# First attention and its projection in one block, with the rotary products in PSUM

## The reference

```python
qkv = x @ Wqkv                                   # q, k, v
q = x_q * cos + rotated(x_q) * sin               # the same for k
att = softmax(where(causal, (q @ k.T) * scale, -inf))
out = (att @ v) @ Wo + bo
x = layernorm(x + out)
```

## Time and profile before

| | us |
|---|---|
| median of three runs | 849.43 (847.52 to 850.48) |
| profiled execution | 850.17 |
| its span, first to last instruction | 848.5 |
| first product on DVE (chunk 0) | 8.97 |
| first product of chunk 6 | 43.06 |
| last piece of the projection on DVE starts | 55.52 |
| first fill on PE | 61.29 |
| first scores of unit 0 | 71.71 |
| DVE busy over the span | 549.5 (65%) |
| PE busy over the span | 663.7 (78%) |

### The profile page before, as it was taken

One profiled execution on the slowest core, in us unless ns is written; L12 is line 12 of the kernel. 1 busy time (PEld: TensorE's weight loads), 2 busy tenths in 40 slices (PEclk: granted clock), 3 DMA queues, 4 the chain that ended last, 5 costly groups with the idle time before them and its releaser, 6 DMA issues. The chain is left out here.

```text
span 848.5 us, 18182 instructions
## 1 busy us (share of the span) xinstructions
PE 663.7 (78%) x6567; PEld 417.8 (49%) x6567; DVE 549.5 (65%) x1564; ACT 439.1 (52%) x658; POOL 409.1 (48%) x597
## 2 busy tenths in 40 slices
PE   6748999999869999999977759999996514988500
PEld 3423555555435666666654436676674203555400
DVE  6977888888558898888896653444546883222115
ACT  5433777777746555555535656676763540232102
POOL 7853777777740000000015765666664603778744
PEclk9975999999979999999998987999998755899765
DMA  4774453432000000000004789889861070354354
GB/s 159 241 228 95 114 176 108 121 85 73 5 1 1 1 1 2 1 1 1 2 0 149 243 277 212 198 181 196 190 150 36 22 204 20 73 128 99 34 91 128
DMA packets 134982, 85.79 MB, mean 101 GB/s; under 512 B 11248, under 2 KB 131568, under 8 KB 134768
## 3 DMA queue, kind: packets, MB, share of 16 engines
q1 hardware_dynamic: 128112, 79.33, 35.0%
q0 software_dynamic: 5632, 4.33, 3.6%
q10 hardware_dynamic: 1152, 0.98, 0.4%
HBM read 54.73 MB, written 29.49 MB: 99 GB/s over the span
## 5 line engine op out<-in xcount | busy, mean ns | idle before, releaser
L2164 ACT ACTIVATE a_prob<-a_ps_pair 128x1024 f32<-128x1024 f32 x96 | 93.1, 1023 | 48.0 <-PE a_ps_pair L2000 36.4
L1835 ACT ACTIVATE a_prob<-a_ps_pair 128x1024 f32<-128x1024 f32 x96 | 96.4, 1023 | 14.8 <-PE a_ps_pair L1638 12.0
L2176 POOL TENSOR_SCALAR_AFFINE_SELECT a_prob<-a_prob 128x512 f32<-128x512 f32 (+1 forms) x96 | 76.7, 807 | 51.0 <-ACT a_prob L2164 50.8
L1876 POOL TENSOR_SCALAR_AFFINE_SELECT a_prob<-a_prob 128x512 f32<-128x512 f32 (+1 forms) x96 | 75.7, 789 | 42.4 <-ACT a_prob L1835 41.8
L1774 DVE TENSOR_REDUCE a_mx<-a_ps_pair 128x4 f32<-128x1024 f32 x64 | 77.8, 1220 | 24.9 <-PE a_ps_pair L1679 23.3
L922 POOL TENSOR_SCALAR xn<-xn,stats,norm_b_rstd 128x128 f32<-128x128 f32 x8 | 6.4, 806 | 175.0 <-POOLq L411 175.0
L478 PEld LDWEIGHTS m_ps_n<-wd,m_act 128*128 128x128 f32 x512 | 66.3, 192 | 29.0 <-issue 27.4
L701 ACT ACTIVATE m_up<-m_ps_u,m_bup 128x512 f32<-128x512 f32 x64 | 44.0, 687 | 65.2 <-PE m_ps_u L466 65.2
L590 DVE SCALAR_TENSOR_TENSOR xn<-m_ps_n,m_wt,xn 128x128 f32<-128x128 f32 x256 | 71.7, 343 | 0.2 <-DVE xn L590 0.2
L478 PE MATMUL m_ps_n<-wd,m_act 128*128 128x128 f32 x512 | 67.5, 275 | 1.0 <-DVE xn L590 0.8
L466 PE MATMUL m_ps_u<-m_x1T,wgu 128*128 128x512 f32 x128 | 66.9, 605 | 0.0
(11 more groups left out here) (295 smaller groups left out, 1535.0 us busy)
## 6 DMA issues: line engine op xcount, KB each, us to landing
qst<-scratch_q SPq DMA_DIRECT2D x64, 128.0 KB, 3.0
kst<-scratch_k SPq DMA_DIRECT2D x64, 128.0 KB, 3.2
scratch_q<-p_parts SPq DMA_DIRECT2D x16, 384.0 KB, 2.4
scratch_k<-p_parts SPq DMA_DIRECT2D x16, 384.0 KB, 2.5
qst<-scratch_q SPq DMA_DIRECT2D x32, 192.0 KB, 3.1
kst<-scratch_k SPq DMA_DIRECT2D x32, 192.0 KB, 3.5
c_w<-in_w SPq DMA_DIRECT2D x8, 578.0 KB, 3.9
scratch_q<-parts SPq DMA_DIRECT2D x16, 256.0 KB, 2.5
```

The lines of the kernel that those rows point to most:

```text
L1835: nc.scalar.activation(prob[:, r % 6, :], pair[(0, 2, 1)[j]][:, :], ACT.Exp, scale=scale, bias=0.0).then_inc(s_e, 1)
L1876: nc.gpsimd.affine_select(out=blk, in_=blk, compare_op=ALU.is_ge, fill=0.0, base=0, pattern=[[0, n], [1, P]], channel_multiplier=-1).then_ ...
L2164: nc.scalar.activation(prob[:, r % 6, :], pair[r % 2][:, :], ACT.Square, scale=scale, bias=1.0).then_inc(s_e, 1)
L2176: nc.gpsimd.affine_select(out=blk, in_=blk, compare_op=ALU.is_ge, fill=0.0, base=0, pattern=[[0, n], [1, P]], channel_multiplier=-1).then_ ...
```

## The change

The function `project_layer0` is gone. Its work stands at the head of the block of `attend_softmax`, with no meeting of the engines in between, and is written out chunk by chunk.

- The pairs of banks of the attention serve the projection too: item n takes pair n mod 3, and the last three items take pairs 2, 1 and 0. Before, q and k had one pair each. v uses the bank `ps_x`.
- The cosine product is written over its own input in PSUM; the sine product goes to SBUF. The sum of an odd item (k) is written over the cosine product too. ACT reads the high level of k from PSUM, and DVE subtracts it there. The sum of an even item (q) goes to SBUF as before, and POOL subtracts.
- The fills, shadings and maxima of unit 0 stand between the last projections; the first unit's split of maxima stands in POOL's last chunk.
- SP loads three stacks within the projection, each after a wait for the stores that it needs, and the store of the last chunk stands behind the third stack.
- The copies of the shading constants, POOL's clearing of `v_now` and its first copy of v move into the chunks.

The core of the diff:

```diff
-AHEAD = 2
+AHEAD = 3
@@ PE
+                project_qk(12)
+                fill(-LEAD, 0)
+                shade(0)
+                project_qk(13)
+                project_v(6)
+                fill(-LEAD, 1)
+                shade(1)
+                project_qk(14)
+                fill(-LEAD, 2)
+                shade(2)
+                project_qk(15)
+                project_v(7)
...
+                    if w == 0:
+                        pe.wait_ge(s_free, (11, 13, 14)[f])
+                    if w == 1 and f < 2:
+                        pe.wait_ge(s_free, 15 + f)
@@ DVE
-                        last = nc.vector.tensor_tensor(
-                            term[:, j, i, :].rearrange("p (b t) -> p b t", b=2),
-                            ps_qk[j][i].rearrange("p (b t) -> p b t", b=2),
-                            rot[:, i, :, :].to_broadcast([P, 2, T]), ALU.mult)
...
-                    nc.vector.tensor_tensor(roped[:, j, :], term[:, j, 0, :], term[:, j, 1, :], ALU.add).then_inc(s_rope, 1)
+                    nc.vector.tensor_tensor(cos, cos, rot[:, 0, :, :].to_broadcast([P, 2, T]), ALU.mult)
+                    nc.vector.tensor_tensor(term[:, n % 2, :].rearrange("p (b t) -> p b t", b=2), sin,
+                                            rot[:, 1, :, :].to_broadcast([P, 2, T]), ALU.mult).then_inc(s_rot, 1)
...
+                        nc.vector.tensor_tensor(roped[:, n // 2 % 2, :], here, term[:, 0, :], ALU.add).then_inc(s_free, 1)
+                    else:
+                        nc.vector.tensor_tensor(here, here, term[:, 1, :], ALU.add).then_inc(s_rope, 1)
...
+                    nc.vector.tensor_tensor(resid[:, 1, :], bank(pair_of[n], 0), level(n, 0), ALU.subtract).then_inc(s_free, 1)
...
+                for c in range(NCH):
+                    rotate(2 * c)
+                    if c > 0:
+                        residual(2 * c - 1)
+                    combine(2 * c)
+                    if c >= 6:
+                        reduce(0, 0 if c == 6 else 2)
+                    rotate(2 * c + 1)
+                    combine(2 * c + 1)
@@ ACT
+                for c in range(NCH):
+                    hi(2 * c)
+                    if c > 0:
+                        mid(2 * c - 1)
+                    hi(2 * c + 1)
+                    mid(2 * c)
+                    copy_v(c)
@@ POOL
+                for c in range(NCH):
+                    if c > 0:
+                        lo(2 * c - 1)
+                    residual(2 * c)
+                    if c == 7:
+                        split_max(0)
+                    lo(2 * c)
+                    if c == 3:
+                        nc.gpsimd.memset(v_now[:, :, :, :, :], 0.0).then_inc(s_vz, 1)
@@ SP
+                    if c < NCH - 1:
+                        store(c)
+                    if 2 <= c < 2 + 2 * AHEAD:
+                        load_stacks(sp, (c - 2) // 2, stacks, scratch, s_store, s_st[(c - 2) // 2], "qk"[c % 2])
+                store(NCH - 1)
```

More of the change, by code:

```diff
@@ L1579, in bank, with level, load @@
             return pair[p][:, 512 * m:512 * m + 512]
+        half_of = [slice(2 * BUFS * i, 2 * BUFS * (i + 1)) for i in range(2)]
+        stack_rows = [st[:, :, :, :].rearrange("p s h t -> p (s h) t") for st in stacks]
+        pair_of = [n % 3 for n in range(13)] + [2, 1, 0]
+        def level(n, i):
+            return parts[:, n % 4, MID_HI_LO[i], :]
+        def load(eng, c):
+            after(eng, s_vp, c - XBUFS + 1)
+            eng.dma_start(xc[:, c % XBUFS, :], io["xT"][:, c * CH:(c + 1) * CH]).then_inc(s_xc[c % XBUFS], 16)
         with nc.Block() as block:
@@ L1734, in project, with project_qk, project_v @@
                     last.then_inc(s_o, 1)
-                for u in range(-LEAD, NU + 2):
+                def project_qk(n):
+                    c, j = n // 2, n % 2
+                    if j == 0:
+                        pe.wait_ge(s_xc[c % XBUFS], 16 * (c // XBUFS) + 16)
+                    if n == 14 or n == 15:
+                        pe.wait_ge(s_mx, n - 13)
+                    else:
+                        after(pe, s_free, 12 if n == 13 else n - 2)
+                    for i in range(2):
+                        last = nc.tensor.matmul(bank(pair_of[n], i), wqk[:, 2 * j + i, :], xc[:, c % XBUFS, :], start=True, stop=True)
+                    last.then_inc(s_proj, 1)
+                def project_v(c):
+                    pe.wait_ge(s_wv, 16)
+                    after(pe, s_vc, c)
+                    for t in range(4):
+                        here = slice(t * P, (t + 1) * P)
+                        last = nc.tensor.matmul(ps_x[:, here], xc[:, c % XBUFS, here], wv[:, :], start=True, stop=True)
+                    last.then_inc(s_vp, 1)
+                pe.wait_ge(s_w, 16)
+                for c in range(6):
+                    project_qk(2 * c)
+                    project_qk(2 * c + 1)
+                    project_v(c)
+                project_qk(12)
+                pe.wait_ge(s_rows, 2)
+                pe.wait_ge(s_rows2, 3)
+                pe.wait_ge(s_tri, 5)
+                fill(-LEAD, 0)
[9 more added lines that the diff above has]
+                project_v(7)
+                for u in range(1 - LEAD, NU + 2):
                     here, ahead, back = 0 <= u < NU, u + LEAD < NU, 0 <= u - 1 < NU
@@ new lines, in combine @@
+                def combine(n):
+                    ve.wait_ge(s_rot, n + 1)
+                    here = bank(pair_of[n], 0)
+                    if n % 2 == 0:
+                        after(ve, s_r1, n // 2 - 1)
+                        after(ve, s_hi, n - 3)
+                        nc.vector.tensor_tensor(roped[:, n // 2 % 2, :], here, term[:, 0, :], ALU.add).then_inc(s_free, 1)
+                    else:
+                        nc.vector.tensor_tensor(here, here, term[:, 1, :], ALU.add).then_inc(s_rope, 1)
@@ new lines, in residual @@
+                def residual(n):
+                    ve.wait_ge(s_hi, n + 1)
+                    after(ve, s_lo, n - 1)
+                    nc.vector.tensor_tensor(resid[:, 1, :], bank(pair_of[n], 0), level(n, 0), ALU.subtract).then_inc(s_free, 1)
+                nc.vector.memset(v_all[:, :, :, HD:HV], 1.0).then_inc(s_zero, 1)
+                nc.vector.memset(ones_sq[:, :], 1.0).then_inc(s_zero, 1)
+                ve.wait_ge(s_crow, 16)
+                nc.vector.tensor_copy(stack_rows[1][:, half_of[0], :], crow[:, 1:2, :].to_broadcast([P, 2 * BUFS, T])).then_inc(s_rows, 1)
@@ L1810, in _ @@
+                reduce(1, 0)
+                residual(2 * NCH - 1)
+                reduce(1, 1)
+                reduce(1, 2)
+                for u in range(2 - LEAD, NU + 2):
                     b = (u - 3) // 2 if u % 2 == 1 and u >= 3 else None
```

325 lines of the change are left out of this document (124 added, 201 removed).

## The result

The changed kernel takes 840.21 us, the median of 4 runs (839.49 to 840.72), against 849.11 (847.52 to 850.48, 4 runs): a ratio of 0.9895, 95% interval 0.9876 to 0.9915, so faster, clear of the noise. Forecast were 840.5 us. Its profiled execution took 840.72 (span 839.0).

A forecast was written before the change was run, and what follows sets the result against it. DVE's queue and the idle hole from 53 to 61 us were taken to set the time up to 71.7 us. First scores at 62.0 save 9.7 us, so 850.17 becomes 840.5 us, range 836.0 to 846.5.

The forecast's parts named there:

- The hole closes, and the sign follows: Between projection and maxima, PE's idle stretch from 53 to 61 us goes; kernel faster, 88%.
- DVE's cheaper chunk: Projection: seven DVE instructions with one PSUM input, 4.5 us a chunk instead of 5.4; POOL three subtractions of 1.17.
- fourth rival: DVE writes PSUM at half speed: 24 writes, 11.6 us lost against 9.7 gained, 852.1 us; chance 5%.
- Loop of two chunks, 10.4 us: Projection: chain through ACT, POOL, PE and DVE takes 10.4 us per two chunks, 5.2 a chunk.
- the clearing, priced at 0.85: POOL's 1.80 us memset, now after chunk 3's even low part, costs 0.85 us beyond POOL's free 0.95.
- The rows of the maxima, issued at 58.3 us: SP issues them behind the last store, whose two issues take 0.9; first scores at most 4.2 us later.
- the first rival: SP's queue and transfers hold chunks 2 to 5 at 5.8 us: 842.9, up to 847 if stack 0 is late; 18%.
- Slow clock in the last chunk: Last k projection at half speed takes 3.6 us instead of 1.8, fills 0.25 more each: 842.7 us; chance 17%.
- the signs of being right: No DVE idling over 1.2 us between 40 and 62; sums 0.6 to 0.7, subtractions 1.17, products 5.2 apart, scores at 62.
- First scores 62.0, gain 9.7: Attention's first scores start at 62.0 us instead of 71.7, which saves 9.7 us.
- Nothing else moves: After the first scores, unit spacing, tail and later stages keep the same instructions, so the gain there is kept unchanged.

The follow-up runs named there:

- the first of the two last copies: Changed kernel with third stack's k loads behind x and maxima rows, casts on ScalarE, POOL's clearing before its first wait: median 840.04 us, ratio 0.9880 to 0.9935.
- the third execution: Changed kernel, unedited, profiled a third time: 840.02 us, first scores at 63.78; median of its runs 841.11 us.
- the second execution of the kernel before: Kernel before, unedited, profiled once more: 849.86 us in one run, first scores at 71.80, attention's last weighted sum at 237.01.
- the second queue copy: Changed kernel, SP issuing last store, first maxima rows, x's first part, second rows, then third stack's k loads: median 841.67 us, ratio 0.9887 to 0.9935.
- first queue copy: Changed kernel with the third stack's k loads moved behind the first maxima rows: median 844.56 us, ratio 0.9925 to 0.9953.

## Why the prediction was right, point by point

- *The hole closes, and the sign follows.* Right and shown: without the interleaving PE stands 9.38 us and most of the gain at the first scores is gone.
- *DVE's cheaper chunk.* Right: 0.68 to 0.70 us an instruction, POOL at 1158 ns, 15 to 19 ns for writing PSUM (fourth rival dead). That the operands' place matters is shown by the product in SBUF; in two chunks without casts it is worth 0.5 us there, of the 1.4 by which two chunks got shorter.
- *Loop of two chunks, 10.4 us.* Right where neither casts nor clearing stand in it: 10.60 and 10.20 in the first of the two last copies (chunk 4 at 28.98, chunk 6 at 39.18). Missed: the casts, 2.9 us in all, which made the loop of chunks 2 and 3 take 12.14, while the clearing, priced at 0.85, cost nothing behind them. With only the casts gone it does cost: 11.34 from chunk 4 to 6 (29.20 to 40.54). That chunk 6 was only 0.4 off is luck: against the 1.7 of the casts stood the clearing's 0.85, a chunk 2 at 18.06 and not 18.4, and 0.2 in the second loop.
- *The rows of the maxima, issued at 58.3 us.* This is the step that failed. I set 0.9 for the store's issues and forgot the loads that stand ahead of them: they end at 58.59, and only then the store's two parts go, 2.38 and 1.01, so the rows came to 62.12 (60.95 in the third execution). The loads are only part of these 3.8 us: in the three copies that move them the rows still go out at 60.36 to 61.07. The last low part came at 58.97 and not at 57.4, behind the slow last k, and the k part alone took 0.90 to 2.07 to issue in those copies. In the last copy without spare matmuls the low part was done at 57.12 and the rows went at 58.10, as the forecast had it. It is the first rival's place, though not its mechanism: chunks 2 to 5 were not held up.
- *Slow clock in the last chunk* (second rival): it happened, 3.13 us for the last k. Here it was hidden behind that queue: with the last k at 1.98, in the copy with spare matmuls and in that with the casts on ScalarE, the first scores still came at 65.09 and 64.68. It also broke one of the signs of being right: DVE idled 1.82 us ahead of 53.32, where at most 1.2 was to be seen.
- *First scores 62.0, gain 9.7.* Mis-sized: 63.8 to 65.0, so 6.7 to 8.0.
- *"Nothing else moves".* Wrong in size. In the first profiles, where the spans differ by 9.5 us, 6.8 come at the first scores, 1.2 from the clock, which is back 9.5 us after the first scores and not 12.3, and 0.6 and 1.3 from the two chance events of the kernel before; 0.4 is lost behind. Against the second execution of the kernel before, the clock's share is 0.5 to 0.7. So the total of 840.5 agreed partly by luck: these made up for 2.9 us that were missing at the first scores.

What stays open: why the same two store issues take 1.11 us in one execution and 2.38 in another, what decides whether the clock falls after a wait, and what makes the part behind the attention vary by 3 us.

## What to carry to other kernels

When work is drawn between the last steps of a stage, list for each in-order queue, DMA issue above all, what stands ahead of the row that the next stage waits for, with its issue times; and before a load is put back, find who waits for what is now queued behind it. Where two fillers lie one behind the other in a loop, taking one out only uncovers the other. Compare such edits at the end of their stage if the rest of the program varies by more than they can win.

## What the hardware showed that was not expected

- The clock fell in the middle of dense work: from 50 to 52 us, after PE had waited 1.98 us, 0.71, 0.79 and 0.53 of full speed were granted in the three executions of the changed kernel, and 1.00 in the second queue copy after the same wait. The Trainium skill (TensorE: Matmul & The Clock Gate, Part 1) says of the change to the full clock that its moment varies from run to run; these rows show the same of the fall.
- A wait of about 1 us can cost more than itself: after 1.01 us at 105.95 the clock fell to 0.58 (first queue copy), after 0.58 us at 98.71 in the last copy without spare matmuls it stayed at 1.00. The length of the wait alone doesn't decide it: after 1.48 at 75.97 in the second queue copy the clock stayed at 1.00 too.
- Casts from SBUF into SBUF on DVE took 214 ns each in the hole of the kernel before, and 569 and 866 in the changed kernel, with POOL at work.
